# Second mixture of experts: two chosen experts for each token in sorted tiles, instead of all eight

## What is computed

```python
def _L1_ffn_ref(x, Wr, br, W1, b1, W2, b2):        # x: (4096, 128), 8 experts, hidden 256
    logits = xf @ Wr + br
    topk_w, topk_idx = jax.lax.top_k(logits, 2)
    topk_w = jax.nn.softmax(topk_w, axis=-1)
    gate = jnp.sum(jax.nn.one_hot(topk_idx, 8) * topk_w[..., None], axis=1)
    h = jax.nn.relu(jnp.einsum('th,ehf->etf', xf, W1) + b1[:, None, :])
    y = jnp.einsum('etf,efh->eth', h, W2) + b2[:, None, :]
    out = jnp.einsum('te,eth->th', gate, y)
...
x = x + 0.5 * _L1_ffn_ref(_layernorm(x), ...)      # first mixture
x = x + _L1_attn_ref(_layernorm(x), ...)
x = x + 0.5 * _L1_ffn_ref(_layernorm(x), ...)      # second mixture
```

## Time and profile before

| What | Value |
|---|---|
| Time, median of 3 runs | 1620.76 us (1620.44 to 1622.02) |
| Time of the profiled execution | 1617.13 us |
| Its span, first to last instruction | 1615.4 us |
| Mean TensorE clock granted, of full speed | 0.946 |
| PE, DVE, ACT, POOL busy | 87%, 62%, 54%, 26% |

### The profile page before, as it was taken

The page is one execution under the profiler, slowest core; times in us unless marked ns, Lnnn a source line. Parts: engine busy times, 40 slices in busy tenths (PEclk is TensorE's granted clock), DMA queues, the critical chain, the costliest instruction groups (busy, mean ns, idle before and its releaser), DMA issues. The chain is left out here.

```text
span 1615.4 us, 37203 instructions
## 1 busy us (share of the span) xinstructions
PE 1412.7 (87%) x11945; PEld 980.0 (61%) x11945; DVE 1005.8 (62%) x3167; ACT 878.3 (54%) x1559; POOL 424.8 (26%) x709
## 2 busy tenths in 40 slices
PE   2688888888769999997899969999799997999998
PEld 1466666666547777775555545555455555777776
DVE  2477887787636767676456555666566665545553
ACT  2466666666424434442577747777566664334343
POOL 4355565565310000111233322323222220000000
PEclk9799999999869999998799989999899998999999
DMA  5312222322100000000445543454344440000000
GB/s 130 79 51 70 78 51 66 78 60 68 32 2 1 11 11 10 11 15 23 121 122 135 126 115 94 116 133 120 87 117 121 103 118 23 8 8 13 6 6 13
DMA packets 62787, 102.97 MB, mean 64 GB/s; under 512 B 7942, under 2 KB 51934, under 8 KB 53470
## 3 DMA queue, kind: packets, MB, share of 16 engines
q1 hardware_dynamic: 62686, 101.76, 25.3%
HBM read 80.60 MB, written 20.97 MB: 63 GB/s over the span
## 5 line engine op out<-in xcount | busy, mean ns | idle before, releaser
L1126 ACT ACTIVATE e_buf<-ps_q 128x1024 f32<-128x1024 f32 x192 | 196.2, 1022 | 113.8 <-PE ps_q L1741 113.8
L1633 PEld LDWEIGHTS ps_o<-w,e_buf 128*128 128x128 f32 x2048 | 241.5, 192 | 23.1 <-issue 21.0
L1633 PE MATMUL ps_o<-w,e_buf 128*128 128x128 f32 x2048 | 250.6, 276 | 0.0
L2306 DVE SCALAR_TENSOR_TENSOR e_buf<-ps_o,gate,e_buf 128x128 f32<-128x128 f32 x512 | 144.0, 344 | 121.7 <-PE ps_o L1633 120.1
L1752 PE MATMUL ps_o<-e_buf,v_st 128*32 128x256 f32 x3072 | 208.8, 390 | 0.2
L1126 ACT ACTIVATE e_buf<-ps_k 128x1024 f32<-128x1024 f32 x192 | 195.5, 1018 | 13.8 <-PE ps_k L1741 12.0
L1062 ACT ACTIVATE e_buf<-ps_q,b_t 128x512 f32<-128x512 f32 x128 | 87.6, 686 | 147.7 <-PE ps_q L1625 145.9
L2047 DVE TENSOR_REDUCE mx<-ps_q 128x6 f32<-128x768 f32 x128 | 121.8, 952 | 64.8 <-PE ps_q L1340 63.8
L1062 ACT ACTIVATE e_buf<-ps_k,b_t 128x512 f32<-128x512 f32 x128 | 87.2, 687 | 131.7 <-PE ps_k L1625 130.0
L2520 DVE COPY o_sb<-ps_o 128x256 f32<-128x256 f32 x192 | 81.0, 422 | 107.8 <-PE ps_o L1752 64.8
L1741 PE MATMUL ps_q<-q_st,k_st 73*128 73x256 bf16 x768 | 121.4, 282 | 30.3 <-DMA q_st<-scr_q 18.2
(11 more groups left out here) (323 smaller groups left out, 2644.4 us busy)
## 6 DMA issues: line engine op xcount, KB each, us to landing
q_st<-scr_q SPq DMA_DIRECT2D x64, 576.0 KB
k_st<-scr_k SPq DMA_DIRECT2D x192, 192.0 KB
scr_q<-parts SPq DMA_DIRECT2D x64, 192.0 KB, 2.1
scr_k<-parts SPq DMA_DIRECT2D x96, 64.0 KB
out_dram<-x SPq DMA_DIRECT2D x8, 256.0 KB, 2.3
w<-in_L_ffn_W_dram SPq DMA_DIRECT2D x1, 1024.0 KB
e_buf<-in_L_attn_w_qkv_dram SPq DMA_DIRECT2D x1, 192.0 KB
k_st<-k_const SPq DMA_DIRECT2D x2, 56.0 KB
```

Of the source, the lines that this page charges most:

```text
L1126: act.activation(e_buf[g % 2][:, hp * 2 % HG:hp * 2 % HG + 2, :], (ps_q, ps_k)[hp % 2][:, :, :], ACT.Exp).then_inc(sem("fast_exp"), 1)
L1633: last = mm(ps_o[:, e % 2, t * P:(t + 1) * P], h_sb[e % 2][:, f, t * P:(t + 1) * P], w2[:, e * NF + f, :], start=f == 0, stop=f == NF - 1)
L2306: last = stt(acc[u][:, t, :], ps_o[:, e % 2, t * P:(t + 1) * P], gate[u][:, t, e:e + 1], acc[u][:, t, :], ALU.mult, ALU.add)
```

## The change

The second mixture is written anew; the first keeps its form. It now runs over four chunks of four batches (`NC`), eight tiles of tokens each.

- DVE ranks the experts as before and marks the two chosen ones (`sel`). PE counts with products of `sel` by constant matrices how many tokens before each one chose the same expert (`positions`). From this DVE works out (`slots`) a slot for each token and choice, so that the tokens of an expert stand together and each expert starts at a new tile of 128; the owner of each tile (`expert`); and the weights of the two choices, halved.
- A chunk has 16 full tiles of choices, and up to 7 more for the experts' partly filled last tiles: 23 tiles (`SLOTS`) are computed, whatever the numbers say.
- POOL scatters the normed tokens to `slots_in` in DRAM: 16 indirect DMAs of 128 rows per chunk (`send`). SP loads them in "quads" of four tiles (`load_quad`).
- For each tile PE makes a transpose of the rows, one product of 256 columns by the owner's first layer, two transposes of the result, a product that sets the second bias from three bfloat16 parts, and two products by the second layer. ACT copies the transposed rows (four tiles at a time) and the product, and applies the bias and relu in two instructions of 128x128. PE and ACT each read the owner from SBUF to a register (`value_load`).
- DVE copies a quad of results to SBUF (`quad_out`), SP stores it to `slots_out`, POOL gathers the rows with 16 indirect DMAs per chunk (`fetch`), and DVE adds them with their weights to `x` (`collect`), 16 instructions of 128x128 per chunk.
- The norm, logits and ranks of a chunk are done two chunks ahead, in the tile loop. Those of groups 1, 2 and 3 stand in front of it.
- Ahead of the attention, POOL makes eight constants more, and SP fills the four `slots_in` with zeros (23 x 128 rows of 512 bytes each) and stores the bias parts.
- `mix_gates(NG, 0)` falls away at the end of `fast_focus`. Some semaphores are merged (`_st` into `_mom`, `_ln` into `_rstd`, `F_er` into `F_ln`, `ml_hi` and `ml_mid` into `ml_cast`); their waits stand where they stood. `gate` now shares memory with `rank` and `lexp`.

```diff
+SLOTS = 2 * CT + EXP - 1
...
             redo_causal(sp, general_causal)
+            sp.wait_ge(sem("consts"), CONSTS + 7)
...
+            for i in range(NC):
+                sp.dma_start(slots_in[i].rearrange("(i p) c -> p i c", p=P),
+                             blank.unsqueeze(1).broadcast_to([P, SLOTS, C])).then_inc(sem("stored"), 16)
...
+            for c in range(NC):
+                sp.wait_ge(sem(f"sent_{c % 2}"), (c // 2 + 1) * 2 * CT * 16)
...
+                load_quad(c, 0)
+                load_quad(c, 1)
+                for q in range(QUADS):
+                    if q + 2 < QUADS:
+                        load_quad(c, q + 2)
+                    store_quad(c, q)
+                if c:
+                    results(2 * c - 2)
+                    results(2 * c - 1)
...
+            def send(c):
+                pool.wait_ge(sem("D_slots"), c * 2 + 2)
...
+                for t in range(CT):
+                    for k in range(2):
+                        pool.indirect_dma_start(
+                            slots_in[c], bass.IndirectOffsetOnAxis(ap=slot_no[c][:, k, t:t + 1], axis=0),
+                            normed_rows(c * 2 + t // GT)[:, t % GT, :], None).then_inc(sem(f"sent_{c % 2}"), 16)
...
+            send(0)
+            send(1)
+            for c in range(NC):
+                if c:
+                    for w in range(CT // 2):
+                        fetch(c - 1, w)
+                if c + 2 < NC:
+                    send(c + 2)
+            for w in range(CT // 2):
+                fetch(NC - 1, w)
...
+            def tile_relu(c, i):
+                j = c * SLOTS + i
+                e = act.value_load(expert[c][0:1, i:i + 1], min_val=0, max_val=EXP - 1)
+                act.wait_ge(sem("E_ht"), j + 1)
+                for f in range(NF):
+                    last = act.activation(h_chan[:, j % 4, f, :], tile_bank(j)[:, (NF + f) * P:(NF + f + 1) * P],
+                                          ACT.Relu, bias=b1_t[:, bass.ds(e * NF + f, 1)])
+                last.then_inc(sem("M_relu"), 1)
...
+                for i in range(SLOTS):
+                    if i % QT == 0 and i // QT + 1 < QUADS:
+                        quad_rows(c, i // QT + 1)
+                    if i + 3 < SLOTS:
+                        at.append(tile_owner(c, i + 3))
+                        tile_hidden(c, i + 3, at[i + 3])
+                    if i + 1 < SLOTS:
+                        tile_turn(c, i + 1)
+                    tile_out(c, i, at[i])
...
+            def collect(c, w):
+                j = c * (CT // 2) + w
+                dve.wait_ge(sem(f"back_{w % 2}"), (j // 2 + 1) * 64)
+                for k in range(2):
+                    for t in range(2 * w, 2 * w + 2):
+                        row = of_group(c * 2 + t // GT)(t % GT)
+                        last = stt(row, y_back[:, t % 4, k, :], weight[c][:, k, t:t + 1], row, ALU.mult, ALU.add)
...
-            mixture_groups(dve, lambda g, u: mixture(g, u, NG, False))
```

More of the change, by code:

```diff
@@ L27 @@
 VW = 32
+CB = 4
+CT = CB * NT
+NC = B // CB
+SLOTS = 2 * CT + EXP - 1
+QT = 4
+QUADS = (SLOTS + QT - 1) // QT
 MIN_SIZE, MAX_ITER = 64, 3
@@ L556, in macaron_kernel @@
+            results(NG - 2)
+            results(NG - 1)
+            sp.wait_ge(sem("stored"), 16 * (NC + 3 + 1 + NG))
         n_loads = 16 * len(SETUP_DMAS)
@@ L1955, in _, with positions @@
             any_path(pe, fast_focus, general_focus)
-            mixture_groups(pe, lambda g, u: mixture(g, u, NG, False))
+            def positions(c):
+                pe.wait_ge(sem("M_step"), past("M_step", c * 29 + 14))
+                w = CT * EXP
+                mm(ps_m[:, 0, 0:w], ahead_b, sel.rearrange("p t e -> p (t e)"), start=True, stop=False)
+                for t in range(CT - 1):
+                    mm(ps_m[:, 0, (t + 1) * EXP:w], ones_b[:, 0:P],
+                       sel[:, t, :].unsqueeze(1).broadcast_to([P, CT - 1 - t, EXP]), start=False, stop=t == CT - 2)
+                for t in range(CT):
+                    last = mm(ps_m[:, 0, w:w + EXP], ones_b[:, 0:P], sel[:, t, :], start=t == 0, stop=t == CT - 1)
+                last.then_inc(sem("M_lg"), 1)
@@ new lines, in quad_rows, with tile_owner @@
+            def quad_rows(c, q):
+                k = c * QUADS + q
+                pe.wait_ge(sem(f"tile_in_{k % 2}"), (k // 2 + 1) * 16)
+                if k:
+                    pe.wait_ge(sem("M_gtc"), past("M_gtc", k))
+                for t in range(in_quad(q)):
+                    last = tr(ps_k[:, 1, t * P:(t + 1) * P], xs[:, k % 2, t, :])
+                last.then_inc(sem("M_gt"), 1)
+            def tile_owner(c, i):
+                return pe.value_load(expert[c][0:1, i:i + 1], min_val=0, max_val=EXP - 1)
@@ new lines, in tile_out @@
+            def tile_out(c, i, e):
+                j, k, t = c * SLOTS + i, c * QUADS + i // QT, i % QT
+                if t == 0:
+                    pe.wait_ge(sem("M_comb"), past("M_comb", max(k - 1, 0)))
+                to = ps_o[:, k % 2, t * P:(t + 1) * P]
+                mm(to, ones_b[0:3, 0:P], b2_rows[:, bass.ds(e, 1), :].rearrange("p e c -> p (e c)"), start=True, stop=False)
+                pe.wait_ge(sem("M_relu"), past("M_relu", j + 1))
+                for f in range(NF):
+                    last = mm(to, h_chan[:, j % 4, f, :], w2[:, bass.ds(e * NF + f, 1), :].rearrange("p e c -> p (e c)"),
+                              start=False, stop=f == NF - 1)
+                if i % QT == in_quad(i // QT) - 1:
+                    last.then_inc(sem("M_out"), 1)
@@ L1985, in ln_stats @@
                 for t in range(tiles):
[L1986 to L1987 removed]
+                    dve.bn_stats(st[:, t, :], src(t)).then_inc(named(pre, "_mom"), 1)
+                dve.wait_ge(named(pre, "_mom"), n * tiles * 2 + tiles)
                 hold()
@@ new lines, in front @@
+            def front(g):
+                mix_stats(NG + g, g)
+                if g >= 4:
+                    dve.wait_ge(sem(f"sent_{g // 2 % 2}"), (g // 4) * 2 * CT * 16)
+                mix_norm(NG + g, g, "M", normed_rows(g))
+            dve.wait_ge(sem("consts"), CONSTS + 8)
+            front(1)
+            mix_ranks(NG + 1)
+            slots(0)
+            front(2)
+            front(3)
+            mix_ranks(NG + 2)
+            mix_ranks(NG + 3)
+            slots(1)
+            for c in range(NC):
+                ahead = c + 2 < NC
+                g = 2 * c + 4
+                if ahead:
+                    front(g)
+                    front(g + 1)
+                quad_out(c, 0)
+                if ahead:
+                    mix_ranks(NG + g)
+                if c:
+                    collect(c - 1, 0)
+                quad_out(c, 1)
+                if ahead:
+                    mix_ranks(NG + g + 1)
+                if c:
+                    collect(c - 1, 1)
+                quad_out(c, 2)
+                if ahead:
+                    slots(c + 2)
+                quad_out(c, 3)
+                if c:
+                    collect(c - 1, 2)
+                quad_out(c, 4)
+                if c:
+                    collect(c - 1, 3)
+                quad_out(c, 5)
@@ L2858 @@
+            for w in range(CT // 2):
+                collect(NC - 1, w)
 _INS = ['L0_attn_x', 'L0_attn_w_qkv', 'L0_attn_w_proj', 'L0_ffn_W_r', 'L0_ffn_W_k', 'L0_ffn_W_v', 'L0_ffn_mu_r',
```

312 lines of the change are left out of this document (272 added, 40 removed).

## The result

The changed kernel takes **1625.97 us** (median of 20 runs, 1621.03 to 1632.24); the kernel before, run beside it, 1620.6 (20 runs, 1612.78 to 1628.33). The ratio is 1.0038, 95% interval 1.0023 to 1.0054: slower by 5.4 us. Forecast were 1632, and slower with 0.57. So the two profiles differ by 14.8 us where the medians differ by 5.4, and single times are compared here only inside a stage.

The account below looks back on a forecast made before the run. TensorE's work bounded the old stage; its instruction queue was to set the new tiles' pace. 46.4 + 171.8 + 18.9 + 30.7 = 267.8 against 256.5 us, 11.3 more: 1632 us, 8-in-10 range 1599 to 1672.

Parts of the forecast that it names:

- Ahead of the first tile: Second mixture's start, before the first product: norm, ranks, counting, slots, 16 POOL DMAs at 1.3 and first load; 46.4 us.
- The tiles: Tile loop of the four chunks: 1.55 us a tile, 41.2 a chunk with fill and clock, 171.8 with two groups' fronts.
- The queue's 1.44: TensorE's instruction queue per tile: register read and operations plus some 20 matrix instructions and weight loads, 1.44 us against array 1.27.
- The first rival: Tile loop: register work runs beside queued products, a tile costs 1.30; 1609, or 1599 with indirect DMAs at 1.0; chance 0.34.
- The clock: Start of each chunk: 3 us lost because PE's clock rises only some 5 us after PE becomes full.
- DVE's work in a chunk: Tile loop: norms, ranks, slots, copies and additions take 30 us in 41, covered by the tiles.
- The joints: Three breaks between chunks, the first load standing behind the last store: 5.7 + 2 x 6.6 = 18.9 us.
- Behind the last tile: End of second mixture: copy, store, 16 gathers, landing, last additions and result out; 30.7 us.
- Hidden: Work said to cost nothing: zero fills in the first mixture (49 us at 123 GB/s), constants, DVE's chunk work, other POOL DMAs.
- The sum: Whole second mixture: 46.4 + 171.8 + 18.9 + 30.7 = 267.8 us against 256.5, 11.3 more.
- One sign that was named: Second mixture: TensorE's busy time would be near 150 us, not 250.
- POOL as the bound: Chunks: from about 1.5 us per indirect DMA, gathers come late and PE stops; 1655 at 1.8 each; chance 0.12.

Follow-up runs that it names:

- the kernel with early loads: Changed kernel with SP issuing the next chunk's first two loads ahead of the last two stores and the results; 1674.0 us, in a later group 1674.6.
- the control: The changed kernel itself, unchanged, run again alone beside the kernel before: 1625.3 us, ratio 1.0059.
- the 1603.4 us version: Changed kernel with SP's next-chunk loads ahead of the last two stores and the bias product over all 128 rows; 1603.4 us, ratio 0.9926 to the kernel before.

## Why the prediction was right, and where not

**Ahead of the first tile**: 44.0 for 46.4. From the attention to the first indirect DMA 17.0 (18.4: the counting products took 0.65, not 1.8); 16 DMAs at 1.26, not 1.3; the rest as worked out. That 1.3 came so close has luck in it: twice SP's 0.61 was a guess, and no run tells what the 1.26 is made of. The experiment with half the chain says that of the whole only some 7.5 us would have come back with eight DMAs fewer, since the counting of chunk 1 stands in TensorE's queue.

**The tiles**: 1.55 each, as forecast, and by the wrong reason. The queue's 1.44 and the measured 1.45 agree by chance: with all register work gone the period did not move. The step that failed is "so the queue is longer than the array ... a tenth above the queue". What stood in its place: an array of 1.16, as the prediction had it without the share of row transposes, with three idle tenths round a product of three rows, of which 0.24 go when it has 128. The first rival ("the array sets the pace") was right about the unit and wrong about its price, since the earlier trace rows hold only products over 128 rows back to back.

The chunks by themselves lasted 42.8, 46.0, 37.8 and 38.6, in sum 165.2 for 171.8. The clock cost what was taken: granted 0.69, 0.78, 0.80 and 0.68 over the first 9 to 10 us of the chunks, 2 to 3 us each. Too dear was the rest, since the last three tiles of a chunk carry no new hidden product (periods of 1.02, 1.02 and 0.82, together 1.5 less). The extra in chunk 1 is a row load that came late: DVE's copy stood behind ranks and four additions, SP's store behind the copy, the load behind the store, and it took 3.83 us to land; the period there is 4.4, and 1.8 at the same tile of the chunk before. In the forecast DVE's work in a chunk was covered and cost nothing.

**The joints**: 23.6 for 18.9. The mechanism was right, and the kernel with early loads shows it; too small was the landing. It was taken as 2.3 from a plain result; rows back from `slots_in` land in 2.9/3.1/4.8 us, the last with two results of 256 KB in front.

**Behind the last tile**: 30.6 for 30.7.

**Hidden.** The zeros went out from 474 and were through by 500, where the DMA share is 0.00; the first key planes start at 545.84. So the cover held with more to spare than the 49 us that were reckoned: the DMAs moved 286 GB/s from 480 to 490, where the forecast had 123. The claim that nothing ahead of the second mixture would move by more than 2 us failed in this profile (7.7 later) and holds on the whole: in the thirteen profiles with the new code the last addition starts from 1358.3 to 1366.2 (mean 1361.9), that of the kernel before at 1358.5 in a run 3.5 below its median. A part of the spread can be seen. In the first mixture TensorE waits at a turn of the loop for DVE, 2.3 to 2.5 us, and the granted clock falls behind some of these waits and not behind others: timeline of PE, the 16 products there in 2.95 us in this profile and in 1.95 in the control.

```profile
587.36 1.12 PE L1458 MATMUL ps_m<-ident,y 128*128 128x128 f32 x4 [2.53 <-DVE y L2285]
588.27 2.95 PE L1831 MATMUL ps_o<-w,e_buf 128*128 128x128 f32 x16
...
585.10 0.66 PE L1458 MATMUL ps_m<-ident,y 128*128 128x128 f32 x4 [2.33 <-DVE y L2285]
585.59 1.95 PE L1831 MATMUL ps_o<-w,e_buf 128*128 128x128 f32 x16
```

The granted clock was 0.70 in the first (588 to 592) and 1.00 in the second. The length of the wait does not decide it: behind the same 2.53 us the 16 products take 1.95 in the second run of the early loads, and behind 2.27 us they take 3.27 at one place of the 1603.4 us version.

**The sum.** 263.3 for 267.8: head -2.4, tiles -6.6, joints +4.7, tail -0.1. The errors have both signs, so the sum is closer than its parts. Against 256.5 that is +6.8, and the medians give +5.4. One sign that was named failed besides: TensorE's busy time is 177 us, not near 150.

**POOL as the bound** did not decide: at 1.26 the chains fit. But the rival saw the right place for another reason. Where the waits beside POOL's chains occur, the changed kernel is at 1678, beyond the range of 1599 to 1672; no row of the kernel before, which has no DMA of POOL, could show them.

## What to carry over

Before a queue or an engine is named as the pace of a loop, add up the array's share and take the other load away: two sums that agree within 1% proved nothing here. A tiny product over a few rows between full ones costs its neighbours' overlap, so a bias is cheaper over all 128 rows, zeros and all: 0.24 us where the array sets the pace, but only 4.5 us in all for the 92 tiles here, since ScalarE and the loads then came last. And a rewrite that trades a full engine for chains (here 75 us at both ends with TensorE nearly idle) gives its gain away there: 73 us of TensorE's work fell off and the kernel got slower, until the joints were closed (21.4 us) and a part of the idle array was taken out (4.5 us).

## What the hardware showed unexpectedly

- Indirect DMAs of 128 rows of 512 bytes issued by POOL: 0.96 us each, 1.26 from start to start. SP goes on 2.2 us after the start of the last scatter of the first chunk; a gather lands 2.5 to 4.3 us after its start, median 2.6.
- A register read from SBUF in TensorE's queue takes 0.302 us (92 of them, 0.295 to 0.606) and in ScalarE's 0.278 with 0.152 behind it, and in a queue that runs ahead of its array it costs nothing: the period stayed 1.45 without them.
- A bf16 product over 3 rows amid products over 128 takes 0.15 from start to start with 0.10 idle ahead of it; over 128 rows 0.06 with none. The Trainium skill, "TensorE: Matmul & The Clock Gate", section "Step-by-step: what each phase is for", says that weights are loaded ahead of products in flight where the row groups do not conflict, or into the background buffer; it also says that the count of rows doesn't matter to the time of the load. The traces agree with the second: the load takes 0.090 us over 3 rows and 0.098 over 128. Of the first they show both cases, a load ahead of its product over 128 rows and none over 3; which of the two conditions is lacking over 3 rows no run here shows.
- The same program took 1625 us or 1678 us, in every run of a group about the one or the other, with the kernel before at 1616 to 1621 in all of them. The difference stands in waits of up to 12 us (up to 17 in other traces) of ScalarE and DVE for TensorE, beside chains of POOL's indirect DMAs.
